# Gate features of the first attention stacked into 96 rows by DMA, with their low parts and the value work reordered

## What is computed

```python
emb  = box_relational_embedding(boxes)          # sin and cos of 100 * log of relative place and size
g    = relu(einsum('bnmd,hd->bhnm', emb, Wg) + bg)
a    = einsum('bhqd,bhkd->bhqk', q, k) / sqrt(64)
mn   = softmax(log(clip(g, 1e-6)) + a)
out  = einsum('bhqk,bhkd->bqhd', mn, v) @ Wo.T + bo
x    = x + tanh(g_xattn[0]) * out
```

## Time and profile before

| | us |
|---|---|
| median of 3 runs | 1161.57 |
| lowest and highest | 1159.33, 1162.9 |
| the profiled execution | 1160.38 |
| its span, first to last instruction | 1158.5 |
| PE busy in the span | 958.8 (83%) |
| first attention, about | 80 to 476 |
| period of one tile, tiles 7 to 8 | 23.6 |

### The profile page before, as it was taken

How to read it: one execution, slowest core, us unless ns; L and a number is a source line. 1 busy time by engine, 2 the same in 40 slices (tenths; PEclk the granted TensorE clock), 3 DMA queues, 4 the chain that set the end, 5 groups by cost and what they waited for, 6 DMA issues and landing times.

```text
span 1158.5 us, 32871 instructions
## 1 busy us (share of the span) xinstructions
PE 958.8 (83%) x12178; PEld 778.2 (67%) x12178; DVE 822.9 (71%) x1947; ACT 683.9 (59%) x1338; POOL 712.6 (62%) x811
## 2 busy tenths in 40 slices
PE   0549999999999974679878469993899999999996
PEld 0346777777777753445554358871799999999995
DVE  3988887788778867468777689966566566666663
ACT  2457888888888863065426368864354444444452
POOL 2988888876776672034512569974566666666672
PEclk9878999999999997589989679985899999999998
DMA  9276776787677755500001000002553225832251
GB/s 285 66 197 138 137 143 157 161 194 151 153 155 143 135 121 137 187 7 1 1 26 44 5 2 21 21 21 92 170 156 94 32 45 166 259 88 32 31 143 14
DMA packets 52117, 119.65 MB, mean 103 GB/s; under 512 B 7616, under 2 KB 30144, under 8 KB 51632
## 3 DMA queue, kind: packets, MB, share of 16 engines
q0 software_dynamic: 14144, 35.48, 21.3%
q1 hardware_dynamic: 35520, 80.71, 20.5%
q10 hardware_dynamic: 2352, 2.10, 0.6%
HBM read 212.54 MB, written 37.85 MB: 216 GB/s over the span
## 4 chain that ended last, share of the span: by engine, by line
PE 51%; DVE 17%; POOL 11%; ACT 9%; issue 6%; DMA 4%; ACTq 0%; SPq 0%; POOLq 0%; DVEq 0%
PE bank L2107 17%; PE bank L2121 9%; POOL PT L560 5%; PE bank L1786 5%; PE bank L1689 3%; ACT EX L1393 2%; PE bank L1728 2%; PE bank L1766 2%; DVE h L1063 2%; DVE nmx L1177 2%; PE bank L1937 2%; ACT L1362 1%; PE bank L1721 1%; PE bank L1899 1%; ACT fks L1362 1%
## 5 line engine op out<-in xcount | busy, mean ns | idle before, releaser
L1623 ACT ACTIVATE yg<-bank,bms 128x128 f32<-128x128 f32 x312 | 105.7, 363 | 113.1 <-PE bank L2107 106.0
L1296 DVE TENSOR_TENSOR hm<-hf,hm 128x256 f16<-128x256 f32 x156 | 66.8, 428 | 99.7 <-ACT hm L1630 94.2
L2107 PE MATMUL bank<-xT,wm_even 128*128 128x128 f16 x1920 | 117.7, 221 | 3.1 <-DVE hf L1291 1.8
L1291 DVE SCALAR_TENSOR_TENSOR hf<-bank,bms,yg 128x128 f32<-128x128 f32 x312 | 98.6, 346 | 26.9 <-ACT yg L1623 25.8
L707 POOL DMA_INDIRECT out_x<-ys,sidx x39 | 62.7, 1608 | 86.2 <-DVE ys L1310 86.2
L2107 PEld LDWEIGHTS bank<-xT,wm_even 128*128 128x128 f16 x1920 | 111.5, 99 | 6.2 <-DVE hf L1291 3.9
L2107 PE MATMUL bank<-xT,wm_odd 128*128 128x128 f16 x1824 | 110.1, 219 | 2.3 <-DVE hf L1291 2.3
L2107 PEld LDWEIGHTS bank<-xT,wm_odd 128*128 128x128 f16 x1824 | 104.2, 98 | 4.9 <-DVE hf L1291 2.4
L1630 ACT ACTIVATE hm<-hf 128x256 f16<-128x256 f32 x156 | 64.6, 414 | 69.0 <-DVE hf L1291 68.2
L560 POOL TENSOR_TENSOR PT<-PT 128x512 f16<-128x512 f32 x64 | 72.3, 1158 | 42.7 <-ACT PT L1419 42.7
L619 POOL TENSOR_TENSOR h<-h 128x512 f16<-128x512 f32 x32 | 40.6, 1281 | 81.8 <-DVE h L1063 79.8
(11 more groups left out here) (308 smaller groups left out, 2658.7 us busy)
## 6 DMA issues: line engine op xcount, KB each, us to landing
wm_even<-expert_weights SPq DMA_DIRECT2D x60, 1024.0 KB
wm_odd<-expert_weights SPq DMA_DIRECT2D x57, 1024.0 KB
expert_weights<-in_wcat POOLq DMA_DIRECT2D x16, 768.0 KB, 8.0
wsp<-expert_weights SPq DMA_DIRECT2D x16, 768.0 KB, 4.3
wsp<-in_wcat POOLq DMA_DIRECT2D x16, 768.0 KB, 10.8
expert_weights<-wsp SPq DMA_DIRECT2D x16, 768.0 KB, 3.3
Lst<-gate_tables SPq DMA_DIRECT2D x48, 68.0 KB, 5.9
gate_tables<-Lw SPq DMA_DIRECT2D x6, 512.0 KB, 4.6
```

The lines of the kernel that those rows point to most:

```text
L1291: v.scalar_tensor_tensor(hf[:, (c // 2) % 2, c % 2, :], bank[c % 4][:, MT:2 * MT], bms[:, par, FC + c:FC + c + 1], yg[:, c % 4, :], ALU.ad ...
L1296: v.tensor_tensor(hm16[:, par, 1, c - 1:c + 1, :], hf[:, q % 2, :, :], hm16[:, par, 0, c - 1:c + 1, :], ALU.subtract).then_inc(m_hl, 1)
L1623: s.activation(yg[:, c % 4, :], bank[c % 4][:, 0:MT], ACT.Gelu, bias=bms[:, par, c:c + 1]).then_inc(m_g, 1)
L2107: ins = t.matmul(bank[c % 4][:, w * MT:(w + 1) * MT], wm16[par][:, wp, col:col + P], xT16[:, par, xp * KD + kk, :], start=(n == 0), stop=( ...
```

## The change

The gate's products change in form. The 16 queries are cut into 4 groups of 4 (`QN`). For each group q, 32 rows (`QR`: two axes, two phases, two frequencies, four queries) of features are stacked three times in the new tile `Fst`: the high part twice and the low part once, 96 rows (`FR`). `We16` holds the high part of the weights, the low part and the high part again, in 96 rows and 64 columns. So the three products of the split are one matmul over 96 rows, and each half of a bank takes four matmuls of 64 columns (written as 16 runs of 4 columns) in place of three of 256.

The stack is made by SP with DMAs from SBUF to SBUF: per tile 8 for the high part (`stack_high`) and 4 for the low part (`stack_low`), each 32 rows of 1024 float16. PE's gate waits for their landing (`gate_features_stacked`). `F16s` and `Fst` have one buffer each. The inputs are laid out anew for this order of rows.

Two orders change. POOL makes the low features between its second and third group of low probabilities. On PE, `pv` waits for each group by itself and is cut into (0, 1) and (2, 3) with the first half of `project_v` between them; the second half of `project_v` is cut in two around `turn_o`. On DVE the wait behind the reciprocal uses another semaphore, with no other effect on the order.

```diff
-        F16s = sb("F16s", [P, 2, 2, NJ * N], F16, l0)
+        F16s = sb("F16s", [P, 2, NJ * N], F16, l0)
+        Fst = sb("Fst", [P, NN // QN, NJ * N], F16, l0)
...
+            def stack_high(b):
+
+                sp.wait_ge(s_fhi, b + 1)
+                if b:
+                    sp.wait_ge(s_gf, 4 * b)
+                for q in range(NN // QN):
+                    for k in range(2):
+                        sp.dma_start(Fst[k * QR:k * QR + QR, q, :], F16s[q * QR:q * QR + QR, 0, :]).then_inc(s_fst, 16)
+
+            def stack_low(b):
+
+                sp.wait_ge(s_flo, b + 1)
+                for q in range(NN // QN):
+                    sp.dma_start(Fst[2 * QR:3 * QR, q, :], F16s[q * QR:q * QR + QR, 1, :]).then_inc(s_fst, 16)
...
                 if b == NJ:
                     store_tables(1)
                 load_tables(b)
+                stack_high(b - 1)
+                stack_low(b - 1)
                 store_half(b // 2 - 1, par)
                 load_half(b // 2, par)
...
-                    probs_low(b - 1)
+                    probs_low(b - 1, (0, 1))
                     feature_low(b, par)
+                    probs_low(b - 1, (2, 3))
...
-                    for n, (wp, fp) in enumerate(PAIRS):
-                        ins = t.matmul(bk[:, jj * 256:(jj + 1) * 256], F16s[:, par, fp, j * N:(j + 1) * N], We16[:, wp, :], start=False,
-                                       stop=(n == 2), skip_group_check=True)
+                    part = bk[:, jj * 256:(jj + 1) * 256].rearrange("p (h q i) -> p q h i", h=H, q=NN // QN)
+                    for q in range(NN // QN):
+                        ins = t.matmul(part[:, q, :, :], Fst[0:FR, q, j * N:(j + 1) * N], We16[0:FR, :], start=False, stop=True,
+                                       skip_group_check=True)
...
-            def pv(c, par, first):
-                pe.wait_ge(s_pl, 4 * c + 4)
+            def pv(c, par, first, fs_=range(4)):
                 pe.wait_ge(s_vl, 2 * c + 2)
-                for f in range(4):
+                for f in fs_:
+                    pe.wait_ge(s_pl, 4 * c + f + 1)
```

More of the change, by code:

```diff
@@ L31 @@
 GW = GL + N
+QN = 4
+QR = 2 * QN * 4
+FR = 3 * QR
+STK = 16 * 3 * (NN // QN)
 WSC = 64.0
@@ L346, in _ @@
             sp.dma_start(boxn[:, :, :], a["boxn"]).then_inc(s_cw, 16)
-            for xy in range(2):
-                for e in range(2):
-                    sp.dma_start((cm, rows)[e][64 * xy:64 * xy + 64, :], a["boxm"][xy, e, :].partition_broadcast(64)).then_inc(s_cw, 16)
+            for e in range(2):
+                sp.dma_start((cm, rows)[e][:, :], a["boxm"][e]).then_inc(s_cw, 16)
             sp.dma_start(bqk[:, :, :], a["bqk"]).then_inc(s_o, 16)
@@ L554, in feature_low, with probs_low @@
                 gp.wait_ge(s_fhi, n + 1)
-                nc.gpsimd.tensor_tensor(F16s[:, par, 1, :], fs, F16s[:, par, 0, :], ALU.subtract).then_inc(s_flo, 1)
-            def probs_low(c):
-                for g in range(4):
+                if n:
+                    gp.wait_ge(s_fst, STK * n)
+                nc.gpsimd.tensor_tensor(F16s[:, 1, :], fs, F16s[:, 0, :], ALU.subtract).then_inc(s_flo, 1)
+            def probs_low(c, gs=range(4)):
+                for g in gs:
                     gp.wait_ge(s_ph, 4 * c + g + 1)
@@ L1363, in feature_sine @@
                 ac.wait_ge(s_fa, 3 * n + 3)
-                if first > 1:
-                    ac.wait_ge(s_gf, 4 * n - 4)
-                s.activation(F16s[:, par, 0, :], fs, ACT.Copy).then_inc(s_fhi, 1)
+                if n:
+                    ac.wait_ge(s_fst, STK * n)
+                s.activation(F16s[:, 0, :], fs, ACT.Copy).then_inc(s_fhi, 1)
             def xn_high(b, par):
@@ L1681, in project_qk, with project_v @@
                     ins.then_inc(s_qf, 1)
-            def project_v(b, par, rs):
+            def project_v(b, par, rs, ns=range(6)):
                 for r in rs:
                     pe.wait_ge(s_qe, 6 * b + r + 1)
-                    n = 0
-                    for (wp, xp) in PAIRS:
-                        for kk in range(KD):
-                            ins = t.matmul(bank[2 + r][:, :], ctx16[:, par, xp, kk, :], wqkv16[:, 2, wp, kk, 512 * r:512 * r + 512],
-                                           start=(n == 0), stop=(n == 5))
-                            n += 1
-                    ins.then_inc(s_qf, 1)
+                    for n in ns:
+                        (wp, xp), kk = PAIRS[n // KD], n % KD
+                        ins = t.matmul(bank[2 + r][:, :], ctx16[:, par, xp, kk, :], wqkv16[:, 2, wp, kk, 512 * r:512 * r + 512],
+                                       start=(n == 0), stop=(n == 5), skip_group_check=True)
+                    if 5 in ns:
+                        ins.then_inc(s_qf, 1)
             def row_scores(b, par, q, first):
@@ L1808, in iteration @@
                 if c:
+                    pv(b - 1, 1 - par, c == 1, (2, 3))
+                if has_q:
+                    project_v(b + 1, 1 - par, (1,), range(3))
+                if c:
                     turn_o(b - 1)
                 if has_q:
-                    project_v(b + 1, 1 - par, (1,))
+                    project_v(b + 1, 1 - par, (1,), range(3, 6))
                 if has_x:
@@ L2169, in arrange @@
             for fr in range(2):
-                for nn in range(NN):
-                    We[xy, sc, fr, nn, :, nn] = feat(sc, xy, fr)
-    a["We"] = We.reshape(P, H * NN)
+                for i in range(QN):
+                    We[:, xy, sc, fr, i, :, i] = feat(sc, xy, fr)
+    a["We"] = We.reshape(FR, H * QN)
     AB = np.zeros((SLOTS, 2, H), np.float32)
```

59 lines of the change are left out of this document (31 added, 28 removed).

## The result

The changed kernel takes 1202.58 us (median of 4 runs, 1200.52 to 1204.01), the kernel before beside it 1160.45: a ratio of 1.036, 95% interval 1.033 to 1.039. Slower was forecast, but 1173 and at most 1187; it is 15.6 us beyond the upper end. The profiled execution has a span of 1201.6 against 1158.5, 43.1 us more.

A forecast was written before the change was run, and what follows sets the result against it. The prediction took a loop through all engines, slightly longer than PE's own program, as the bound. Terms 3.9 + 5.1 + 2.2 + 1.0 = 12.2 us on 1160.38 gave 1172.6, forecast as 1173 on the runs' scale; range 1156 to 1187.

The forecast's parts named there:

- The steady tile: Iterations 2 to 14 of the first attention: the loop through all engines grows 0.3 us a tile, 3.9 us in all.
- The delay of the fourth group: In `pv`: POOL's low features put ahead make DVE finish normalising O's last group at P + 7.92, not P + 7.61.
- rival 4: PE idles about 3 us a tile, its clock halves and `project_o` slows: 36 us more, 1209; chance 0.06.
- Gaps stay under 2 us: Argument against a clock drop: PE's idle gaps stay this short in all tiles but the eighth (index 7).
- Tile 7: PE's gate waits 4.1 us for stack DMAs queued behind table stores and loads, plus 1.0 for lower clock: 5.1 us.
- The start: Iteration 0: twelve stack DMAs on SP precede first table stores and weight loads; costs 1.0 us, between 0 and 5.
- The cover named: In iteration 0, PE's existing 4.95 us wait behind its first gate hides most of SP's 5.0 us of stack issues.
- The end: Iteration 15: low stack ahead of SP's last store and feed-forward weights delays them and DVE by 2.2 us (1.0 to 3.5).
- The shorter gates at nothing: PE's gate groups save 1.84 us a tile, but waits for DVE's row maxima and POOL absorb it: 0 us gained.

## Why the prediction was wrong

- **The steady tile, 3.9 us in all: its own part right, a step missing.** The delay of the fourth group was 0.27 to 0.35 against 0.3. The step that failed is the sentence "Everything behind (floor, logarithm, copy of O, `project_o`, scores, exponentials) is in program order on ACT and PE and moves by the same 0.3." The floor did not only move, it grew: by 0.73 to 0.86 in 12 tiles (in the 13th it came later and grew by 0.41). Of the 1.12 that each of the 13 periods gained, 14.6 us, some 11 us are this. It grew because POOL's splits did not move with it: they start 6.57 behind P as before (6.56), while the floor comes at 7.80 (in the first tiles 7.88) instead of 7.53. The sign was in the trace: in the kernel before, the first of these floors comes 1.36 behind the start of the splits and takes 1.47, and all the others come at 0.97 and take 0.73 or 0.74.

```profile
102.40 4.97 POOL L546 TENSOR_TENSOR q<-qt,q 128x512 f16<-128x512 f32 x4
...
103.76 1.47 DVE L846 TENSOR_SCALAR fu<-fu 128x1024 f32<-128x1024 f32 x1
...
128.16 0.74 DVE L846 TENSOR_SCALAR fu<-fu 128x1024 f32<-128x1024 f32 x1
```

- **The clock, rival 4, chance 0.06.** The right mechanism at far too low a chance. "Gaps stay under 2 us" failed with the floor: the gap ahead of the turn of `xn` went from 0.11 to 2.25. 1.1 of that is the later floor; the other 1.0 is the new order itself, in which PE is done with its value products 9.4 behind P instead of 10.4. With the floor at 0.68 the gap was 1.35 to 1.48, and no `project_o` of these tiles was slow. In size the rival was too large (36 us; measured in 6 of 13 tiles, 1.7 each, 10 us).
- **Tile 7, 5.1 us: 6.8 measured.** PE waited 5.95 for the stack, where 4.1 was worked out. The mis-sized term is the issue: it takes 0.59 us at the median, not 0.42, and these twelve took 8.0 us from 264.07 on, not 5.0. The landing that counts, that of the last (issued at 271.09), took 4.82 against the 4.8 taken from another kind of load, so right by luck: over all these copies it is 2.0 to 7.2, median 3.7. The 2.2 that the prediction sets beside it from the Trainium skill (DMA: Bandwidth & Descriptors, section Anatomy of one DMA) is that section's fit for DMAs that GpSimd issues, not SyncE; here it is near only the first of the twelve (2.04).
- **The start, 1.0 us: 5.1 measured,** just over its upper bound of 5. The cover named, PE's wait of 4.95 for ScalarE, covered nothing: PE waited 6.21 for the stack and then still 5.14 for ScalarE, which itself came later, because it waited 5.55 for the expert weights (88.58), whose load stands behind the stacks on SP. And the eight stack copies ahead of the table stores delayed the landing of these too, which was not in the sum.
- **The end, 2.2 us: 2.8 measured.** Right: SP's store goes out 6.95 behind the start of the last tile's low groups instead of 3.87, and VectorE's sum of the feed-forward weights waits for them and starts 2.8 later.
- **The shorter gates at nothing: right.** A group takes 0.66 (0.62 predicted). PE's waits for DVE's row maxima are 17.9 in 14, 1.3 each, where about one was predicted. By the Trainium skill (TensorE: Matmul & The Clock Gate, section LDWEIGHTS) a load of 128 columns takes 107 ns. The trace has 98 ns for a single one at the median (97 in `pv` before), so what the prediction rejected is not the time of one load but the adding up: the loads overlap, and eight products with theirs take 0.41 us, 51 ns each.

Of 39 us in the first attention, 12 were forecast; 21 of the missing 27 are the floor and its clock, 4 the start, 2 tile 7 and the end.

## What to carry to other kernels

When a change moves one engine's work against another's, look at operations of VectorE and GpSimd that overlap, not only at who waits by semaphore: list the durations of each one over all tiles, and take any outlier (here one 1.47 among 0.73) as what a small shift can make the rule. Count PE's gap after the shift too, since a gap that grows from 0.11 to 2.25 can cost the clock behind it. And a wait that is taken off one operation must be followed to the next one that overlaps; here it cost 1.3 us on the update of X.

## What the runs showed of the hardware

- VectorE's floor (128x1024, float32, in place) takes 0.68 us where no split of GpSimd runs. Beside four splits of 1.12 us each, with no issue of GpSimd's ahead of them and but for the tiles of the next point, arrivals from 0.15 to 0.99 ended at 1.70, those from 1.09 to 2.13 at 2.82, one at 2.61 at 3.94 and one at 3.65 at 5.05: each time some 0.58 behind the end of a split.
- With the same arrival (0.83) it ended at 1.70 or at 5.04 from tile to tile, and one at 3.07 ended at 5.05 (the kernels with twelve memsets). With GpSimd's issue of a DMA of its own ahead of the splits, also 2 us ahead, it ended at 5.05 in all 13 tiles of each such kernel; in the tile without that issue, 1.70. Why is open.
- An update with two inputs in SBUF (128x256) took 0.48 us; it took 1.83 when it came 0.85 ahead of the end of one GpSimd split with another behind that, and 0.64 when it came 0.35 ahead of the end of one with none behind.
- `project_o` was slow behind 6 of 13 waits of PE of about 2.25 us, behind 9 of 13 of 2.4, behind none of 0.97, 1.48 or 1.6 in the steady part, and behind each of 4.0 (4.9 to 6.4 us). Where it took 5.41 at 398.85, the granted clock of its window was 0.71.
- A copy of 64 KB from SBUF to SBUF took SP 0.59 us to issue at the median (0.51 to 1.66) and landed after 2.0 to 7.2 us.
